# A cross-attention and expert-FFN kernel: its opening rewritten to take tiles in twos, with the query projected right after the first half of the keys

## The chip, the cores and the metric

The kernel runs on one core of a Trainium2 chip. The metric is the device time of one execution in microseconds (us). The engines are TensorE (PE, with its weight loads as PEld), VectorE (DVE), ScalarE (ACT), GpSimd (POOL) and SyncE (SP), whose queue issues all DMAs of this kernel.

## The reference

```python
x = x + xattn(layernorm(x), ctx)         # x: 4 x 512 x 256, ctx: 4 x 1024 x 256
x = x + ffn(layernorm(x))                # 16 experts of 128, gated by a sigmoid
# xattn: lat = LN(x)*g+b; c = LN(ctx)*g+b; q = lat@Wq; k, v = split(c@Wkv)
#        16 heads of 64; k = rope(k, cos, sin)
#        softmax(clip(q k^T / 8, -11, 11)) v, then @Wo + bo
```

Every product of the projections and of the scores is taken as three fp32r products (hi x hi, hi x lo, lo x hi), so each operand is rounded ("hi") and its remainder kept ("lo").

## The kernel before

The attention phase works on 32 items: 4 batches by 8 pairs of heads ("pair" below always means such a pair of heads, item n). While item n runs, its successor p = n + 1 is prepared. An item has four macro steps m, and in each two of its eight score steps s (128 rows of context against 512 queries, for two heads). Every engine has its own order, written out by hand, and semaphores couple them; nothing is planned by a program.

- **PE** (L912 to L956): in m = 0 the scores 0 and 1 of item n, then the two key halves of item n + 1 (`project_k`), then the last two steps of `attend` (probabilities by values) of item n - 1 and its second `denominators`. In m = 1 scores 2 and 3, `q_product(n + 1)`, half of the values (`project_v`), attend 0 and 1. In m = 2 scores 4 and 5, the transposes of one tile of inputs (`turn_tile`), attend 2 and 3. In m = 3 scores 6 and 7, the other half of the values, attend 4 and 5, the first `denominators`.
- **ACT** (L1093 to L1128): the exponentials of each macro step and the copies out of PSUM; in m = 2 `round_k` and then the `affine` of the tile.
- **DVE** (L1308 to L1350): clips each exponential (L1231), adds them in twos (L1239), takes the statistics of tile t = n + 10 in m = 0, normalises it in m = 1 (L1175, L1178), and right behind that turns the denominators of item n - 1 into inverses (`invert_den`, L166 to L172), then the rope products of item n + 1.
- **SP** (L547 to L589), in this order for item n: `swap_k(n + 1)` (4 DMAs), `load_tile(n + 11)`, for n = 1 the load of `x2_head` and of the gate's weights (3 DMAs, L556 to L558), `turn_den(n - 1)` (4 DMAs from `den` to `den_rows`, L156 to L163), `load_weights`, `store_inv`, `spread_inv`, stores of packed weights. What stands behind a wait of this queue waits too. `load_tile(t)` waits until tile t - 2 has been normalised, which frees its buffer `ctx_raw[t % 2]`; tiles with even t also bring one tile of x into the single `x_raw`.
- **POOL** (L711 to L726): in each item `rstd` (a power, L616), `rope_times` (L668), for the first items `split_weights` and `split_v_weights`, then the hi and lo parts of the tile (L631 to L638).

Before item 0 comes the prologue, which is what the change rewrites. It takes the first ten tiles of context (eight make batch 0) and five tiles of x one by one: statistics and normalisation on DVE (L1241 to L1264), the power on POOL, transposes on PE (`turn_first`, L867), the scale and shift and the hi parts on ACT (`affine_first`, L983), the lo parts on POOL (`split_first`, L618). Between them stand, on PE (L889 to L910), the key half 0 of item 0, the value products 0 and 1, the key half 1, the query, the value products 2 and 3. A key half is copied to SBUF (`evac_k`), its rows are swapped in blocks of 32 by DMA (`swap_half`, L495), multiplied and added (`rope_first`, L670 on POOL and L1212 on DVE), and then rounded and split (`round_k_first`, `split_k_first`). The first scores need the first key half, scores 4 to 7 the second (L823, L828). The weights of items 0 and 1 are rounded on ACT and split on DVE; from item 2 on POOL does both.

## Time and profile before

| | |
|---|---|
| median of three runs | 1074.72 us (1074.5 to 1076.34) |
| the profiled execution: its own time | 1075.38 us |
| its span in the profile | 1073.6 us |
| PE busy | 1019.8 us (95% of the span) |
| DVE busy | 777.9 us (72%) |
| ACT busy | 525.4 us (49%) |
| POOL busy | 354.6 us (33%) |
| mean granted PE clock | 0.992 |

Times in the rows count from the span's start, which is also the zero of all times in the text. The profiled execution took 0.66 us more than the median of the three runs, and 1.78 us more than its own span.

### The profile page before, as it was taken

The numbers are of one execution on the slowest core, as the hardware profiler recorded it, in microseconds if no ns is written. First come the engines' busy times: TensorE is split into PE (matmuls) and PEld (weight loads), VectorE is DVE, ScalarE is ACT, GpSimd is POOL, SyncE is SP. The second block draws the span as 40 slices with busy tenths as digits, with TensorE's granted clock in tenths as the row PEclk, the third lists the DMA queues.
The fourth block names the chain that finished last, engine by engine and source line by source line (L and its number), as shares of the span: only waits on it lengthen the run. The fifth ranks groups of instructions, "written<-read, shape, count | busy, mean of one in ns | idle before, by whom it ended". The sixth has DMA issues, their size and how long they took to land. (4 is left out here: it accounts for less than half of the span.)

```text
span 1073.6 us, 15789 instructions
## 1 busy us (share of the span) xinstructions
PE 1019.8 (95%) x5592; PEld 612.8 (57%) x5592; DVE 777.9 (72%) x1140; ACT 525.4 (49%) x759; POOL 354.6 (33%) x276
## 2 busy tenths in 40 slices
PE   4599999999999999999999999999999878999998
PEld 3455455555555555555555555555554356888886
DVE  5498888877888888888888777778778855545422
ACT  5455455555555555655555555555555532222221
POOL 4464534332323222323222211332111145445443
PEclk9899999999999999999999999999999999999999
DMA  6344223332322232323222223322222354332321
GB/s 170 115 137 115 83 85 99 99 96 78 90 65 89 65 90 70 102 80 95 85 70 85 60 80 91 88 79 80 80 60 61 100 181 181 119 109 89 109 108 40
DMA packets 69371, 101.43 MB, mean 94 GB/s; under 512 B 22000, under 2 KB 44784, under 8 KB 67248
## 3 DMA queue, kind: packets, MB, share of 16 engines
q1 hardware_dynamic: 69296, 100.46, 30.8%
q8 instruction: 43, 0.70, 0.3%
q14 instruction: 32, 0.26, 0.1%
HBM read 70.54 MB, written 10.75 MB: 76 GB/s over the span
## 5 line engine op out<-in xcount | busy, mean ns | idle before, releaser
L1026 ACT ACTIVATE probs<-score_ps 128x1024 f32<-128x1024 f32 x256 | 248.8, 1025 | 202.6 <-PE score_ps L835 202.5
L1231 DVE TENSOR_SCALAR probs<-probs 128x1024 f32<-128x1024 f32 x256 | 233.1, 932 | 142.1 <-ACT probs L1026 142.0
L848 PE MATMUL o_ps<-probs,v_sb 128*64 128x512 f32 x1024 | 249.5, 608 | 0.0
L1239 DVE TENSOR_TENSOR p_sum<-probs 128x1024 f32<-128x1024 f32 x128 | 164.7, 1287 | 3.3
L668 POOL TENSOR_TENSOR k_swap<-k_swap,sin_sb 128x1024 f32<-128x1024 f32 x31 | 89.0, 2870 | 189.9 <-DMA k_swap<-k 189.9
L848 PEld LDWEIGHTS o_ps<-probs,v_sb 128*64 128x64 f32 x1024 | 62.3, 136 | 113.1 <-issue 87.6
L835 PE MATMUL score_ps<-q_hi,k_hi 64*128 64x512 f32 x512 | 114.8, 444 | 1.2 <-DVE k_lo L1210 0.8
L1543 POOL TENSOR_TENSOR act_lo<-act,act_hi 128x512 fp32r<-128x512 f32 x64 | 82.6, 1292 | 99.1 <-ACT act_hi L1691 99.1
L835 PEld LDWEIGHTS score_ps<-q_hi,k_hi 64*128 64x128 f32 x512 | 48.3, 184 | 112.5 <-issue 104.5
L1775 DVE SCALAR_TENSOR_TENSOR act<-h_ps,sel_all 128x512 f32<-128x512 f32 x62 | 42.8, 691 | 94.6 <-PE h_ps L142 82.8
L1691 ACT CAST act_hi<-act 128x512 fp32r<-128x512 f32 x64 | 39.7, 622 | 139.5 <-DVE act L1775 139.5
L835 PE MATMUL score_ps<-q_lo,k_hi 64*128 64x512 f32 x512 | 101.4, 391 | 0.0
L835 PE MATMUL score_ps<-q_hi,k_lo 64*128 64x512 f32 x512 | 101.2, 390 | 0.0
L616 POOL TENSOR_TENSOR rstd_sb<-var_sb,power 128x2 f32<-128x2 f32 x32 | 30.8, 961 | 164.0 <-DVE var_sb L1165 96.3
L631 POOL CAST wide_hi<-ctx_t 128x256 fp32r<-128x256 f32 x22 | 24.0, 1093 | 157.9 <-ACT x_t L979 80.5
L142 PE MATMUL job_ps<-wv_hi,wide_hi 128*128 128x256 f32 x240 | 70.8, 295 | 0.0
L863 PE MATMUL side_ps<-p_sum,ones 128*32 128x512 f32 x512 | 68.2, 604 | 0.4 <-DVE yT L218 0.4
L142 PE MATMUL job_ps<-wv_hi,wide_lo 128*128 128x256 f32 x240 | 67.9, 283 | 0.0
L142 PE MATMUL job_ps<-wv_lo,wide_hi 128*128 128x256 f32 x240 | 67.8, 282 | 0.0
L142 PE MATMUL job_ps<-wide_hi,w_hi 128*128 128x512 f32 x128 | 55.1, 430 | 2.8 <-POOL wide_lo L621 2.8
L835 PEld LDWEIGHTS score_ps<-q_lo,k_hi 64*128 64x128 f32 x512 | 48.3, 184 | 11.1
L1018 ACT CAST k_hi<-k 128x1024 fp32r<-128x1024 f32 x31 | 32.5, 1049 | 40.4 <-DVE k L1205 40.4
(196 smaller groups left out, 1898.0 us busy)
## 6 DMA issues: line engine op xcount, KB each, us to landing
sel_all<-sel_dram SPq DMA_DIRECT2D x16, 1024.0 KB, 5.0
k_swap<-k SPq DMA_DIRECT2D x124, 128.0 KB, 2.3
w_hi<-packs_hi SPq DMA_DIRECT2D x26, 384.0 KB, 3.9
w_lo<-packs_lo SPq DMA_DIRECT2D x26, 384.0 KB, 4.4
den<-inv_dram SPq DMA_DIRECT2D x64, 128.0 KB, 2.8
ctx_raw<-ctx SPq DMA_DIRECT2D x24, 128.0 KB, 2.2
packs_hi<-w_hi SPq DMA_DIRECT2D x8, 384.0 KB, 3.3
packs_lo<-w_lo SPq DMA_DIRECT2D x8, 384.0 KB, 3.6
```

What stands on the lines that cost most here:

```text
L142: mm = pe.matmul(out, lhsT, rhs, start=start and i == 0, stop=stop and i == len(terms) - 1)
L668: pool.tensor_tensor(k_swap[:], k_swap[:], sin_sb[:], ALU.mult).then_inc(k_times, 1)
L835: mm = pe.matmul(score_ps[s % 2][:, h, :], k[par][rows, s * P:(s + 1) * P], q[par][rows, :], start=(i == 0), stop=(i == len(terms) - 1))
L848: mm = pe.matmul(o_ps[DH * h:DH * h + DH, :], v_sb[n // 2 % 2][:, at:at + DH], probs[s % RING][:, h, :], start=(s == 0), stop=(s == STEPS ...
L863: mm = pe.matmul(side_ps[at:at + QUAD, :], ones[:], p_sum[2 * part + e][:, h, :], start=(part == 0), stop=(part == 1))
L1018: act.copy(k_hi[p % 2][:], k32[:]).then_inc(k_hi_done, 1)
L1026: act.activation(probs[s % RING][:], score_ps[s % 2][:], ACT.Exp, scale=DH ** -0.5).then_inc(exp_done, 1)
L1231: dve.tensor_scalar(probs[s % RING][:], probs[s % RING][:], CLIP_HI, CLIP_LO, ALU.min, ALU.max).then_inc(clipped, 1)
L1239: dve.tensor_tensor(p_sum[m][:], first, second, ALU.add).then_inc(summed_up, 1)
L1543: pool.tensor_tensor(act_lo[e % ARING][:], act32[e % ARING][:], act_hi[e % ARING][:], ALU.subtract).then_inc(act_split, 1)
L1691: act.copy(act_hi[e % ARING][:], act32[e % ARING][:]).then_inc(act_hi_done, 1)
L1775: dve.scalar_tensor_tensor(out=act32[e % ARING][:], in0=h_ps[e % ARING][:], scalar=0.0, in1=gates[:, at:at + 512], op0=ALU.max, op1=ALU.mu ...
```

## The change

Five changes go together. (1) The first ten tiles of context are handled as five twos ("duos"), with one semaphore step for each: two tiles of context, and in duos 0 and 1 also two tiles of x, so that the four tiles of x that batch 0 needs come in the first two duos. Transposes fill whole banks, and `affine_first` and `split_first` work on blocks of 256 columns twice, or 512 elements in one instruction. (2) The fifth tile of x, which came with tile 8, now comes with tile 11 (`LATE_X`), within item 1; `load_tile(11)` and `load_tile(12)` therefore wait until the tile before them has been normalised as a whole. (3) The order on PE is: duos 0, 1 and 2 turned, value product 0, key half 0, the query, duo 3, value product 1, key half 1, value products 2 and 3. (4) The fifth duo is turned, scaled, rounded and split within item 0 on PE, ACT and POOL, and the second key half is rounded within item 0. (5) DVE takes over the rounding of item 0's weights from ACT; on SP the value weights are loaded behind tiles 4 to 7, the swap of key half 0 goes ahead of the loads of the next weights, and the swap of key half 1 goes behind those loads and the stores of the packed weights.

```diff
--- before
+++ after
...
+LATE_X = 11
...
+FIRST_DUOS = FIRST_TILES // 2
...
+    u = t - FIRST_TILES
+    return u + (u + 1) // 2 + (1 if t > LATE_X else 0)
...
+
+        first_cn = [x2_head[:, 2 * i:2 * i + 2, :] for i in range(2)]
+        first_xn = [t[:].rearrange("p (i d) -> p i d", d=D) for t in (den, o_raw)]
+        first_ct = [yT[:, 0, i * NQ:(i + 1) * NQ].rearrange("p (k n) -> p k n", k=KT) for i in range(2)]
+        first_xt = [yT[:, 1, i * NQ:(i + 1) * NQ].rearrange("p (k n) -> p k n", k=KT) for i in range(2)]
 
         key_raw = [w_raw, w_raw, k_swap, cos_sb]
...
+        def x_index(tile):
+
+            return STEPS // 2 if tile == LATE_X else tile // 2
+
         def x_at(t, tile):
 
-            i = tile % STEPS // 2
-            return t[:, tile // STEPS % 2, :, i * P:(i + 1) * P]
+            i = x_index(tile)
+            return t[:, i // PER % 2, :, i % PER * P:(i % PER + 1) * P]
 
         def has_x(tile):
 
-            return tile % 2 == 0
+            return tile % 2 == 0 or tile == LATE_X
...
+        def duo_x(d):
+
+            return d < PER // 2
...
+        def duo_banks(d):
+
+            if d < 2:
+                return score_ps[d][:, 0, :], score_ps[d][:, 1, :]
+            return (o_ps if d == 2 else side_ps)[:], None
...
+            if f < 2:
+                return score_ps[1][:, f, :]
             if f < FILLS:
...
             def load_tile(t):
 
                 if t >= FIRST_TILES:
-                    sp.wait_ge(normed, blocks(t - 1))
+                    sp.wait_ge(first_normed, FIRST_DUOS)
+                    wait(sp, normed, blocks(t if t in (LATE_X, LATE_X + 1) else t - 1))
                 sp.dma_start(ctx_raw[t % 2][:], ctx_in[t * P:(t + 1) * P, :]).then_inc(ctx_loaded[t % 2], DMA)
...
+            for i in range(2):
+                two = slice(2 * i, 2 * i + 2)
+                sp.dma_start(rows_c[0][:, two, :], ctx_in[2 * i * P:(2 * i + 2) * P, :].rearrange("(t p) d -> p t d", p=P)
+                             ).then_inc(rows_loaded[i], DMA)
+                sp.dma_start(rows_x[:, two, :], x[2 * i * P:(2 * i + 2) * P, :].rearrange("(t p) d -> p t d", p=P)
+                             ).then_inc(rows_loaded[i], DMA)
+                if i == 0:
+                    sp.dma_start(col_sb[:], cols).then_inc(cols_loaded, DMA)
             load_weights(0)
-            load_v_weights(0)
             sp.dma_start(rows_c[1], ctx_in[4 * P:8 * P, :].rearrange("(t p) d -> p t d", p=P)
                          ).then_inc(rows_loaded[2], DMA)
+            load_v_weights(0)
             for q in range(4):
                 rows = slice(32 * q, 32 * q + 32)
                 sp.dma_start(cos_sb[rows, :], cosT).then_inc(consts_loaded, DMA)
                 sp.dma_start(sin_sb[rows, :], sinT).then_inc(consts_loaded, DMA)
             load_tile(8)
             load_tile(9)
+            swap_half(0)
             load_weights(1)
             load_v_weights(1)
-            swap_half(0)
-            swap_half(1)
             store_pack(0)
             store_v_pack(0)
+            swap_half(1)
             load_tile(FIRST_TILES)
             load_weights(2)
...
+                    sp.wait_ge(first_turned, FIRST_DUOS)
                     sp.dma_start(x2_head[:], x[0:512, :].rearrange("(t p) d -> p t d", p=P)).then_inc(head_loaded, DMA)
...
+            def rstd_first(d):
+
+                pool.wait_ge(first_stats, d + 1)
+                wait(pool, first_normed, d - 1)
+                w = 4 if duo_x(d) else 2
+                pool.tensor_tensor(first_rstd[d % 2][:, 0:w], first_var[d % 2][:, 0:w], power[:, 0:w],
+                                   ALU.pow).then_inc(first_rstd_ready, 1)
...
+            def split_first(d):
+
+                pool.wait_ge(first_hi, d + 1)
+                last = pool.tensor_tensor(duo_cols(ctxT_lo, d), first_ct[d % 2], duo_cols(ctxT_hi, d), ALU.subtract)
+                if duo_x(d):
+                    last = pool.tensor_tensor(xT_lo[:, 0, :, d * DUO:(d + 1) * DUO], first_xt[d % 2],
+                                            xT_hi[:, 0, :, d * DUO:(d + 1) * DUO], ALU.subtract)
+                last.then_inc(first_split, 1)
...
-            for t in range(STEPS):
-                rstd(t)
-                if t >= 2:
-                    split_first(t - 2)
-                if t == 6:
-                    pool.wait_ge(sin_signed, 2)
-                    rope_first(0)
-            split_first(STEPS - 2)
-            rstd(STEPS)
-            split_first(STEPS - 1)
-            rstd(STEPS + 1)
+            rstd_first(0)
+            rstd_first(1)
+            split_first(0)
+            rstd_first(2)
+            split_first(1)
+            rstd_first(3)
+            split_first(2)
+            split_first(3)
+            pool.wait_ge(sin_signed, 2)
+            rope_first(0)
+            rstd_first(4)
             rope_first(1)
...
+                    pe.wait_ge(first_split, FIRST_DUOS if p >= PAIRS else STEPS // 2)
+                    if p >= PAIRS:
+                        pe.wait_ge(tile_split, blocks(STEPS * (p // PAIRS + 1)))
...
-                    pe.wait_ge(tile_split, blocks(STEPS * (2 * j // PAIRS + 1)))
+                    if j >= DUOS:
+                        pe.wait_ge(first_split, FIRST_DUOS)
+                        pe.wait_ge(tile_split, blocks(STEPS * (2 * j // PAIRS + 1)))
...
-                    pe.wait_ge(affine_done, blocks(FIRST_TILES))
+                    pe.wait_ge(v_stored, 2)
...
+            def turn_first(d):
+
+                pe.wait_ge(first_normed, d + 1)
+                c_bank, x_bank = duo_banks(d)
+                for bank, rows in ((c_bank, first_cn[d % 2]), (x_bank, first_xn[d % 2])):
+                    if bank is not None:
+                        for k in range(KT):
+                            for i in range(2):
+                                tr = pe.transpose(bank[:, (2 * k + i) * P:(2 * k + i + 1) * P],
+                                                  rows[:, i, k * P:(k + 1) * P], ident[:])
+                tr.then_inc(first_turned, 1)
...
-            for t in range(5):
-                turn_first(t)
-            pe.wait_ge(tile_split, blocks(4))
+            turn_first(0)
+            turn_first(1)
+            turn_first(2)
+            pe.wait_ge(first_split, 1)
+            pe.wait_ge(wv_split, 1)
+            pe.wait_ge(first_affine, 2)
+            v_product(0, 0)
+            pe.wait_ge(first_split, 2)
             pe.wait_ge(w_split, 1)
             k_product(0, 0)
-            turn_first(5)
-            pe.wait_ge(wv_split, 1)
-            v_product(0, 0)
-            turn_first(6)
+            q_product(0)
+            turn_first(3)
             v_product(0, 1)
-            turn_first(7)
-            pe.wait_ge(tile_split, blocks(8))
+            pe.wait_ge(first_split, 4)
+            pe.wait_ge(q_split, 1)
             k_product(0, 1)
-            pe.wait_ge(k_evac, 1)
-            q_product(0)
-            turn_first(STEPS)
-            pe.wait_ge(v_stored, 1)
             v_product(0, 2)
-            turn_first(STEPS + 1)
-            pe.wait_ge(v_stored, 2)
+            pe.wait_ge(first_affine, 4)
             v_product(0, 3)
...
+                    if n == 0 and m == 1:
+                        pe.wait_ge(v_stored, FILLS)
+                        turn_first(FIRST_DUOS - 1)
...
+            def affine_first(d):
+
+                act.wait_ge(first_turned, d + 1)
+                wait(act, first_split, d - 1)
+                c_bank, x_bank = duo_banks(d)
+                for k in range(KT):
+                    last = act.activation(first_ct[d % 2][:, k, :], c_bank[:, k * DUO:(k + 1) * DUO], ACT.Identity,
+                                          bias=b_ctx[:, k:k + 1], scale=g_ctx[:, k:k + 1])
+                if duo_x(d):
+                    for k in range(KT):
+                        last = act.activation(first_xt[d % 2][:, k, :], x_bank[:, k * DUO:(k + 1) * DUO], ACT.Identity,
+                                              bias=b_lat[:, k:k + 1], scale=g_lat[:, k:k + 1])
+                last.then_inc(first_affine, 1)
+                act.wait_ge(first_affine, d + 1)
+                last = act.copy(duo_cols(ctxT_hi, d), first_ct[d % 2])
+                if duo_x(d):
+                    last = act.copy(xT_hi[:, 0, :, d * DUO:(d + 1) * DUO], first_xt[d % 2])
+                last.then_inc(first_hi, 1)
...
-            affine_first(0)
-            affine_first(1)
-            round_weights(0)
-            affine_first(2)
-            affine_first(3)
-            round_v_weights(0)
-            affine_first(4)
-            evac_k(0, 0)
-            affine_first(5)
-            store_v(0, 0)
             def round_k_first(half):
                 act.wait_ge(k_roped, half + 1)
                 act.copy(k_half(k_hi[0], half), k_half(k32, half)).then_inc(k_hi_done, 1)
 
-            affine_first(6)
+            affine_first(0)
+            affine_first(1)
+            affine_first(2)
+            store_v(0, 0)
+            evac_k(0, 0)
+            round_q(0)
+            affine_first(3)
             store_v(0, 1)
+            evac_k(0, 1)
             round_k_first(0)
-            affine_first(7)
-            evac_k(0, 1)
-            round_q(0)
-            affine_first(STEPS)
             store_v(0, 2)
+            store_v(0, 3)
             round_weights(1)
-            store_v(0, 3)
-            affine_first(STEPS + 1)
-            round_k_first(1)
...
+                    if n == 0 and m == 0:
+                        round_v_weights(1)
+                        round_k_first(1)
+                    if n == 0 and m == 1:
+                        affine_first(FIRST_DUOS - 1)
...
+            def stats_first(d):
+
+                slot, width = d % 2, 4 if duo_x(d) else 2
+                if d < 2:
+                    dve.wait_ge(rows_loaded[d], 2 * DMA)
+                elif d < FIRST_DUOS - 1:
+                    dve.wait_ge(rows_loaded[2], DMA)
+                else:
+                    for i in range(2):
+                        dve.wait_ge(ctx_loaded[i], DMA)
+                rows = duo_rows(d)
+                if duo_x(d):
+                    rows = rows + [rows_x[:, 2 * d + i, :] for i in range(2)]
+                for i in range(width):
+                    last = dve.bn_stats(first_bn[slot][:, i, :], rows[i])
+                last.then_inc(first_bn_done, 1)
+                dve.wait_ge(first_bn_done, d + 1)
+                for i in range(width):
+                    last = dve.bn_aggr(first_mv[slot][:, i, :], first_bn[slot][:, i, :])
+                last.then_inc(first_aggregated, 1)
+                dve.wait_ge(first_aggregated, d + 1)
+                wait(dve, first_rstd_ready, d - 1)
+                last = dve.tensor_scalar(first_var[slot][:, 0:2], first_mv[slot][:, 0:2, 1], EPS, None, ALU.add)
+                if duo_x(d):
+
+
+                    last = dve.tensor_scalar(first_var[slot][:, 2:4], first_mv[slot][:, 2:4, 1], 1.0 + EPS, EPS * EPS,
+                                             ALU.mult, ALU.add)
+                last.then_inc(first_stats, 1)
...
+            def normalize_first(d):
+
+                slot = d % 2
+                dve.wait_ge(first_rstd_ready, d + 1)
+                wait(dve, first_turned, d - 1)
+                for i, rows in enumerate(duo_rows(d)):
+                    last = dve.tensor_scalar(first_cn[slot][:, i, :], rows, first_mv[slot][:, i, 0:1],
+                                             first_rstd[slot][:, i:i + 1], ALU.subtract, ALU.mult)
+                if duo_x(d):
+                    for i in range(2):
+                        last = dve.tensor_scalar(first_xn[slot][:, i, :], rows_x[:, 2 * d + i, :],
+                                                 first_mv[slot][:, 2 + i, 0:1], first_rstd[slot][:, 2 + i:3 + i],
+                                                 ALU.subtract, ALU.mult)
+                last.then_inc(first_normed, 1)
+
+            def round_weights():
+
+                dve.wait_ge(w_loaded, 3 * DMA)
+                dve.tensor_copy(w_hi[0][:], w_raw[:, 0:WC]).then_inc(w_hi_done, 2)
+                split_weights(0)
+
+            def round_v_weights():
+
+                dve.wait_ge(wv_loaded, DMA)
+                dve.tensor_copy(wv_hi[0][:], wv_raw[:]).then_inc(wv_hi_done, 1)
+                split_v_weights(0)
...
-                    rope_first(1)
+            stats_first(0)
+            normalize_first(0)
+            stats_first(1)
+            normalize_first(1)
+            stats_first(2)
+            round_weights()
+            normalize_first(2)
+            stats_first(3)
+            round_v_weights()
+            normalize_first(3)
+
+            dve.wait_ge(consts_loaded, 8 * DMA)
+            for q in (0, 2):
+                rows = slice(32 * q, 32 * q + 32)
+                dve.tensor_scalar(sin_sb[rows, :], sin_sb[rows, :], -1.0, None, ALU.mult).then_inc(sin_signed, 1)
+            split_q(0)
+            stats_first(4)
+            rope_first(0)
+            split_k_first(0)
+            normalize_first(4)
+            rope_first(1)
             split_weights(1)
             split_k_first(1)
             split_v_weights(1)
                             invert_gate(dve, sh, 0, 0)
...
+                            wait(dve, turned, t - FIRST_TILES)
                             normalize(t, ctx_n[:], x_n[:])
                         if n > 0:
                             invert_den(dve, sh, n - 1)
...
```

## Rows read from the trace of the kernel before

**Rows 1.** Busy time by stretch: us of PE, PEld, DVE, ACT, POOL; then PEclk, DMA share, GB/s.

```profile
0.00:25.00 25.00, 9.75 (x33) 7.12 (x34) 15.29 (x59) 13.33 (x32) 13.36 (x25) 1.00 0.65 175
25.00:50.00 25.00, 13.91 (x69) 11.85 (x69) 10.61 (x22) 10.00 (x23) 10.10 (x11) 0.80 0.32 101
50.00:75.00 25.00, 23.13 (x140) 13.49 (x137) 22.93 (x29) 16.03 (x26) 16.70 (x14) 1.00 0.51 167
200.00:825.00 625.00, 625.00 (x3624) 343.75 (x3622) 502.54 (x675) 347.63 (x475) 154.40 (x98) 1.00 0.28 82
```

**Rows 2.** PE in order of time: start, us of the group, what, count, idle before.

```profile
8.15 0.66 PE L751 MATMUL score_ps<-ident,x_head 128*128 128x128 f32 x2 [8.15 <-DVE den L1178]
8.61 0.63 PE L754 MATMUL score_ps<-ident,den 128*128 128x128 f32 x2
...
22.96 0.56 PE L142 MATMUL o_ps<-wv_hi,wide_hi 128*128 128x256 f32 x1
25.66 0.42 PE L751 MATMUL score_ps<-ident,x_head 128*128 128x128 f32 x2
...
34.95 0.80 PE L142 MATMUL job_ps<-wide_hi,w_hi 128*128 128x512 f32 x1 [2.17 <-POOL wide_lo L621]
...
46.25 0.69 PE L751 MATMUL score_ps<-ident,x_head 128*128 128x128 f32 x2 [4.35 <-DVE x_head L1175]
49.43 0.59 PE L835 MATMUL score_ps<-q_hi,k_hi 64*128 64x512 f32 x2
```

**Rows 3.** DVE in order of time, prologue and item 0.

```profile
3.34 0.43 DVE L1150 BATCH_NORM_STATS2 bn_c<-probs 128x6 f32<-128x256 f32 x1 [3.34 <-DMA p_sum<-x]
3.68 0.41 DVE L1152 BATCH_NORM_STATS2 bn_x<-p_sum 128x6 f32<-128x256 f32 x1
...
44.37 1.10 DVE L1219 TENSOR_TENSOR k<-k,k_swap 128x512 f32<-128x512 f32 x1
...
53.51 0.27 DVE L1270 MEMSET sel_lo<- 128x256 f32 x1
...
60.41 2.48 DVE L1175 TENSOR_SCALAR ctx_n<-ctx_raw,mv_c,rstd_sb 128x256 f32<-128x256 f32 x1
```

**Rows 4.** POOL in order of time.

```profile
11.67 0.72 POOL L621 TENSOR_TENSOR wide_lo<-x_head,wide_hi 128x256 fp32r<-128x256 f32 x1 [1.54 <-ACT xT_hi L992]
13.69 1.36 POOL L621 TENSOR_TENSOR wide_lo<-x_head,wide_hi 128x256 fp32r<-128x256 f32 x1
59.95 2.79 POOL L668 TENSOR_TENSOR k_swap<-k_swap,sin_sb 128x1024 f32<-128x1024 f32 x1 [1.27 <-DMA k_swap<-k]
```

**Rows 5.** Stretches of 2 us, columns as in the first group.

```profile
4.00:6.00 2.00, 0.00 (x0) 0.00 (x0) 0.61 (x6) 0.00 (x0) 0.71 (x1) 1.00 1.07 367
46.00:48.00 2.00, 1.75 (x8) 1.75 (x9) 1.06 (x2) 0.00 (x0) 0.04 (x1) 0.56 0.20 68
118.00:120.00 2.00, 2.00 (x6) 0.48 (x4) 1.97 (x4) 0.60 (x1) 0.00 (x0) 0.50 0.03 4
```

**Rows 6.** SP's DMA issues within item 1, first and last of nine.

```profile
80.70 0.58 SPq L445 DMA_DIRECT2D ctx_raw<-ctx  x1
...
83.31 2.46 SPq L163 DMA_DIRECT2D den_rows<-den  x4
```

**Rows 7.** The tile `den_rows`: from issue to landing, over 12 DMAs.

```profile
DMA to landing us min/median/max: 1.8/1.9/2.8
```

**Rows 8.** DVE within item 1.

```profile
87.90 1.91 DVE L1175 TENSOR_SCALAR ctx_n<-ctx_raw,mv_c,rstd_sb 128x256 f32<-128x256 f32 x1
89.73 0.15 DVE L170 TENSOR_TENSOR inv_rows<-den_rows 128x8 f32<-128x8 f32 x1
92.40 1.29 DVE L1231 TENSOR_SCALAR probs<-probs 128x1024 f32<-128x1024 f32 x2
```

**Rows 9.** PE within item 1 and at the start of item 2.

```profile
95.32 1.94 PE L848 MATMUL o_ps<-probs,v_sb 128*64 128x512 f32 x8
98.18 0.50 PE L835 MATMUL score_ps<-q_hi,k_hi 64*128 64x512 f32 x2
```

129 lines of the change are left out of this document (42 added, 87 removed).

## The prediction

> **What bounds the kernel now.** I read the stretches first [rows 1]. From 200 to 825 us PE is busy all 625 us at full clock, so there a microsecond is neither won nor lost by the opening: whatever item 2 starts earlier or later should come out at the end. In the first 50 us PE is busy 23.7 us (9.75 + 13.91), much of it slowly. That is what the change can win from. PE in order of time [rows 2] shows the opening as one long chain: first transposes at 8.15, value product 0 at 22.96 (12 matmuls in 2.7 us, to 25.66), key half 1 at 34.95 (6 matmuls of 512, as many columns in all), an idle 4.35 us before 46.25 while DVE ropes key half 1, and the first scores at 49.43. The second thing to see is that DVE, not PE, paces item 0: it has 22.93 us of work in the 25 us from 50 [rows 1]. So I follow DVE too: its last preparation ends at 53.7 and it normalises tile 10 at 60.41 [rows 3].
>
> **Part 1, duos up to the first product.** The first duo needs 512 KB where two transfers of 128 KB were enough. Data for the old first tile was there at 3.34 [rows 3]; the stretch from 4 to 6 us moves 367 GB/s [rows 5], so 256 KB more take 0.7 us, and I take 4.8 with the extra issues. DVE: four statistics 0.34 us apart [rows 3] and the small ones, 2.05 in all; POOL's power, 0.75, which has no cover now, since DVE's next statistics stand behind the normalisation; four normalisations, 1.4: 9.0. Eight transposes at twice the 1.1 us of four [rows 2]: 11.1. ACT's four affines of 256 columns have no row. Those of 128 come 0.35 apart; between the same and double I take 0.45, 1.9 us together, then two casts of 512 elements, 1.1 us: 14.2. POOL's two splits of 512 elements: one of 256 takes 0.72 alone and 1.36 beside DVE's weight split [rows 4], so 2.6 alone, and with DVE's weight work beside them 3.8: 18.0. Then the power of duo 2 (0.7), which stands behind that split, DVE's normalisation of duo 2 (20.7, held by POOL's next split), statistics of duo 3, and the value weights, rounded and split by DVE: 23.1. The two casts that DVE takes over have no row there either: between 0.3 and 1.0 us each, near the DVE operations of their size, 0.7 taken. ACT's saving of them costs nothing, for ACT waits there.
>
> So value product 0 starts at 23.1, as before (22.96). **The gain comes behind it.** Key half 0 follows directly (as many columns at the same pace, 2.6 taken, to 28.4), the query (1.8, to 30.2), duo 3, value product 1 (to 32.1). Duo 3 goes through ACT (32.4) and POOL (33.7), key half 1 takes 1.4 at full clock (35.1), value products 2 and 3 1.4 each: 37.9. The first key half is swapped by 33.1, roped by 35.9, split by 37.2, all within that. The first scores at 37.9 against 49.43 [rows 2].
>
> **Part 2, the second key half and item 0.** Its copy is ready at 35.7. SP has by then issued the 4 weight loads and 4 stores it is moved behind; their 1.9 MB take 5.2 us at the rate above, from 31.5 to 36.9, and 8 issues of about half a microsecond. I put its landing at 40.2. Rope: DVE done at 42.3, against 45.5 (44.37 + 1.10 [rows 3]). Then the weight split of item 1 (43.2), ACT's rounding of the half, its split (43.9), value weights, memsets: DVE is free for item 0 at 45.2 against 53.8, 8.6 us earlier. PE waits for item 1's weights from about 40 to 43.2. After its idle 4.35 us the clock stood at 0.56 from 46 to 48 [rows 2, 5]; if this gap does the same, the two key halves of item 1 take up to 5.2 us instead of 2.8, the query is late, and so are duo 4 on ACT and POOL, behind which stand POOL's power of tile 10 and its rope product. Then DVE reaches tile 10 at 54.2, 6.2 us earlier; without it, 8.5. The added transposes (0.5 us), affines and split of duo 4 cost PE nothing while DVE paces. I take a gain of **7.5**, with 5.5 and 9.5 as ends.
>
> **Part 3, the x tile that moves to item 1.** The work only moves: 0.5 us of statistics, which fall into an idle of DVE, and one normalisation. The wait does not. `load_tile(12)` now waits on SP until tile 11 is normalised as a whole, which DVE does in m = 1 of item 1. Behind it in SP's queue stand the three head loads and the four transfers of `turn_den(0)`; and the next instruction on DVE is `invert_den(0)`, which waits for those four. In the old frame: DVE ends tile 11 at 89.7, with x at 90.4 [rows 8]. SP then issues what took it from 80.70 to 85.77, 5.07 us [rows 6], and the last of the four transfers lands some 1.9 behind its issue [rows 7]: 97.3. `invert_den(0)` stood at 89.73 [rows 8]: DVE is 7.5 us late, and had no wait there before. Its next clips end at 93.7 [rows 8] and will end at 101.2. PE goes on alone: transposes, attend 2 and 3, scores 6 and 7, value product, to 96.0; attend 4 was at 95.32 [rows 9] and can start when the first of those clips is done, 100.6. PE loses **5.3 us**, idle for 4.6. Item 2's scores (98.18 [rows 9]) come as late: k must be split by DVE, at 103.6. And after an idle of 4.35 us in the opening the clock was low until 49.6, which doubled 3.4 us of work: I add **1.7**, with 0 and 2.9 as ends (the value product at 22.96 was still at half pace after the gaps before it [rows 2], the longest such stretch here). Together 7.0.
>
> **Sum.** -7.5 + 5.3 + 1.7 = -0.5; and the old trace has one more low stretch, 0.50 from 118 to 120 in item 2 [rows 5], behind a short wait for DVE. It cost some 1.7 us and may not come back in another timing; I take off 0.3 for that: -0.8. Against the profiled execution's own 1075.38 that is 1074.6; it ran 0.66 above the median of the runs, so 1073.9 against 1074.72. What a measurement here can tell from no change is about 0.2%, 2.1 us.
>
> **The rule on the shared port.** DVE's normalisation of tile 10, 256 elements, took 2.48 us from 60.41, and POOL's rope product ran from 59.95 to 62.74 [rows 3, 4]: DVE waited it out. The Trainium skill ("SBUF — State Buffer", Who interferes with whom) says as much: a copy, cast or tensor_scalar of DVE in a 2-port mode and a GpSimd operation exclude each other for the whole instruction. This trace agrees, with those 2.48 us. Taken strictly, every normalisation, cast or weight split of the new opening that meets a split of POOL waits for its whole 1.3 us, which is the first rival below with its 1078.7; by the costs above it is 1073.9.
>
> **Rivals.**
> - *The hold in the opening* (slower). POOL's splits double in length, and each now stands where DVE normalises the next duo or rounds weights. I counted one such hold (1.3 us) and 1.2 us on POOL. If duos 2, 3 and the key half each meet two more splits or products, 2.6 us are added before value product 0, and as much around the rope, the gain falls to about 3.0, and 7.0 are lost later: +4.0, so 1078.7. It decides from the point where the gain falls under 4.9. For it: the 1.36 and the 2.48 [rows 3, 4]. Against it: POOL is idle for half of the old opening (13.36 of 25 [rows 1]).
> - *The stall in item 1 is covered* (faster). If DVE's invert isn't held, or PE has more queued than I count, the gain stays: -6 to -9, about -7.5, so 1067.2. Against it: the orders of SP and DVE are fixed, and nine issues behind a wait can't be early. For it: PE's margin, that I could only count to 96.0.
> - *The chain is as costed* (my forecast): from -4.0 to +2.5, 1070.7 to 1077.2.
>
> **How the numbers follow.** Forecast 0.62: of it 0.36 within 0.2%, 0.18 faster, 0.08 slower. The covered stall 0.25, all faster. The hold 0.13: 0.09 slower, 0.04 within. So faster 0.43, same 0.40, slower 0.17. The range leaves out 0.1 at either end: 1067.5 to 1077.5.
>
> **What would show it.** First scores near 38 (35 to 40). Value product 0 near 23. DVE's clip of step 0 near 45, and normalisation of tile 10 near 53. In item 1 SP silent between `swap_k` and `load_tile(12)` until DVE has normalised x of tile 11, then DVE idle some 6.8 us before `inv_rows`, PE idle 4 to 5 us before attend 4, and a low granted clock behind. I am wrong if that idle isn't there, or if scores of item 2 start by more than 3 us earlier than 98.18.

## The result, and the profile after

The changed kernel takes 1078.03 us (median of six, 1077.45 to 1081.56), against 1074.99 for the kernel before in the same session (six, 1074.31 to 1076.72): a ratio of 1.0032, 95% interval [1.0016, 1.0048]. It is slower by some 3.0 us, where 1073.9 had been forecast and the range ended at 1077.5. (A ratio here and below is not exactly the quotient of the two medians, which would be 1.0028.) One run of those below, 1154.91 us of the kernel with a filler, was in a slow state and counts in no ratio. The profiled execution was the longest of the six, 1081.56 with a span of 1079.8. At 841 us it is 2.3 us behind the kernel before and at its end 6.2, so most of what it has above the median arises behind 841 us, and times up to there can be read as they stand.

The stretches of the kernel after, columns as in [rows 1]:

```profile
0.00:25.00 25.00, 7.13 (x30) 5.99 (x31) 17.12 (x48) 9.26 (x17) 12.18 (x19) 1.00 0.54 142
25.00:50.00 25.00, 17.00 (x88) 13.81 (x89) 14.59 (x29) 10.47 (x18) 5.11 (x5) 0.86 0.52 170
...
200.00:825.00 625.00, 623.89 (x3617) 342.97 (x3613) 505.84 (x680) 347.85 (x474) 154.49 (x99) 1.00 0.28 81
...
44.00:46.00 2.00, 1.39 (x3) 1.17 (x4) 2.00 (x5) 0.29 (x1) 0.00 (x0) 0.50 0.12 33
46.00:48.00 2.00, 2.00 (x6) 1.60 (x5) 1.97 (x4) 0.45 (x1) 0.00 (x0) 0.50 0.89 305
...
98.00:100.00 2.00, 2.00 (x6) 0.24 (x2) 2.00 (x3) 2.00 (x5) 1.01 (x1) 0.50 0.72 269
...
122.00:124.00 2.00, 2.00 (x7) 0.27 (x4) 1.98 (x3) 1.19 (x2) 0.00 (x0) 0.50 0.26 96
...
850.00:875.00 25.00, 21.47 (x97) 9.76 (x94) 16.05 (x21) 9.65 (x12) 3.66 (x3) 0.86 0.27 73
875.00:900.00 25.00, 18.42 (x68) 14.38 (x67) 9.99 (x30) 6.06 (x10) 17.04 (x13) 0.80 0.69 236
```

From 200 to 825 us PE is still full (623.89 of 625 us), so the opening's account is closed by then. Three low stretches are to be seen: at 44 to 48, at 98 to 100, and at 122 to 124 us. The third is the old one of item 2, which the kernel before has from 118 to 120 [rows 5]. The last two lines belong to the surplus of this execution: the kernel before had a granted clock of 1.00 in both of those stretches. It is the only one of all twelve traces that had, though, so its end is as much an exception as this one.

PE in order of time, columns as in [rows 2]:

```profile
22.89 0.55 PE L144 MATMUL score_ps<-wv_hi,wide_hi 128*128 128x256 f32 x1 [1.14 <-issue]
...
36.66 0.51 PE L886 MATMUL score_ps<-q_hi,k_hi 64*128 64x512 f32 x2
...
44.61 0.77 PE L144 MATMUL job_ps<-wide_hi,w_hi 128*128 128x512 f32 x1 [6.28 <-issue]
...
49.87 0.51 PE L886 MATMUL score_ps<-q_hi,k_hi 64*128 64x512 f32 x2
...
69.93 0.51 PE L886 MATMUL score_ps<-q_hi,k_hi 64*128 64x512 f32 x2 [0.76 <-DVE k_lo L1327]
...
97.10 3.38 PE L899 MATMUL o_ps<-probs,v_sb 128*64 128x512 f32 x8 [4.23 <-DVE probs L1348]
100.41 1.26 PE L914 MATMUL side_ps<-p_sum,ones 128*32 128x512 f32 x8
101.60 0.50 PE L886 MATMUL score_ps<-q_hi,k_hi 64*128 64x512 f32 x2
```

The same stations in the kernel before, as far as [rows 2] do not have them:

```profile
72.96 0.51 PE L835 MATMUL score_ps<-q_hi,k_hi 64*128 64x512 f32 x2 [0.77 <-DVE k_lo L1210]
...
97.19 1.07 PE L863 MATMUL side_ps<-p_sum,ones 128*32 128x512 f32 x8
```

Read against the kernel before: value product 0 at 22.89 (22.96), first scores at 36.66 (49.43, so 12.8 earlier), scores of item 1 at 69.93 (72.96, 3.0 earlier), scores of item 2 at 101.60 (98.18, 3.4 later). Three stations: 12.8 won; 9.8 of it gone within item 0 (5.3 of these because DVE reaches its first clip only 7.5 earlier; the forecast had 2.9 of that, 11.5 against 8.6); another 6.4 gone within item 1. What is left is a kernel that is 3.4 late. The first `denominators` of item 1, the line at 100.41, come 3.2 us later than in the kernel before. In the item near 232 us it is still 3.2 (235.25 against 232.03), and in the one near 841 us 2.3 (841.02 against 838.74). I use the line of item 1 as milestone **D1** below (before 97.19, after 100.41), since it stands behind both losses.

DVE and POOL, columns as in [rows 3, 4]:

```profile
41.14 1.78 DVE L1334 TENSOR_TENSOR k<-k,cos_sb 128x512 f32<-128x512 f32 x1 [4.46 <-DMA k_swap<-k]
...
43.56 0.95 DVE L1301 TENSOR_TENSOR w_lo<-w_raw,w_hi 128x768 fp32r<-128x768 f32 x1
...
46.18 1.22 DVE L1348 TENSOR_SCALAR probs<-probs 128x1024 f32<-128x1024 f32 x2
...
51.94 0.69 DVE L1348 TENSOR_SCALAR probs<-probs 128x1024 f32<-128x1024 f32 x1 [2.02 <-ACT probs L1092]
...
54.90 0.69 DVE L1312 TENSOR_TENSOR q_lo<-job_ps,q_hi 128x512 fp32r<-128x512 f32 x1 [1.35 <-ACT q_hi L1071]
...
57.42 2.45 DVE L1229 TENSOR_SCALAR ctx_n<-ctx_raw,mv_c,rstd_sb 128x256 f32<-128x256 f32 x1 [0.59 <-POOL rstd_sb L656]
...
86.69 0.40 DVE L1232 TENSOR_SCALAR x_n<-x_raw,mv_x,rstd_sb 128x256 f32<-128x256 f32 x1
93.67 0.17 DVE L172 TENSOR_TENSOR inv_rows<-den_rows 128x8 f32<-128x8 f32 x1 [6.59 <-DMA den_rows<-den]
...
96.36 1.29 DVE L1348 TENSOR_SCALAR probs<-probs 128x1024 f32<-128x1024 f32 x2
```

```profile
54.46 1.29 POOL L669 TENSOR_TENSOR wide_lo<-yT,wide_hi 128x512 fp32r<-128x512 f32 x1 [12.09 <-ACT wide_hi L1055]
55.70 1.68 POOL L656 TENSOR_TENSOR rstd_sb<-var_sb,power 128x2 f32<-128x2 f32 x1
57.35 2.36 POOL L716 TENSOR_TENSOR k_swap<-k_swap,sin_sb 128x1024 f32<-128x1024 f32 x1
```

SP's issues, in the opening and in item 1, columns as in [rows 6]:

```profile
30.45 0.59 SPq L494 DMA_DIRECT2D w_raw<-Wq  x1
...
34.20 1.21 SPq L525 DMA_DIRECT2D v_packs_lo<-wv_lo  x1
35.46 3.87 SPq L539 DMA_DIRECT2D k_swap<-k  x4
...
75.20 2.42 SPq L548 DMA_DIRECT2D k_swap<-k  x4
87.16 0.34 SPq L484 DMA_DIRECT2D ctx_raw<-ctx  x1
...
89.98 2.45 SPq L165 DMA_DIRECT2D den_rows<-den  x4
```

**Item 1 went as forecast.** SP is silent from the swap at 75.20 until `x_n` of tile 11 is done, some 87.1; nine issues follow; the four transfers of `turn_den(0)` are the last; DVE's `inv_rows` waits 6.59 us for them; the clips that attend 4 waits for move to 96.36, PE is idle 4.23 and then goes at half clock.

**Item 0 did not.** DVE was to be free for the clip of step 0 at 45.2 and is at 46.18, 7.5 earlier than before. But from there to tile 10 DVE took 11.2 us where it had taken 6.7, from this line of the kernel before to 60.41 [rows 3]:

```profile
53.71 1.22 DVE L1231 TENSOR_SCALAR probs<-probs 128x1024 f32<-128x1024 f32 x2
```

The lines of the changed kernel name the waits: 2.02 for ACT's probabilities, 0.22 for the next, 1.35 for ACT's `q_hi`, 0.59 for POOL's power, 4.2 together. They lead back to PE, whose keys of item 1 began at 44.61. PE's row names no releaser for its 6.28 us, but the split of their weights ends on DVE just before (`w_lo`, 43.56 and 0.95). It stands behind the rope on DVE, and the rope behind the swap on SP. An experiment below tests this.

### The profile page after: what moved, and what is told of

It reads as the page before. It is cut to its first block and busy times, and to the rows that moved or that the text cites. A ratio compares the mean times of both kernels' runs of the same rounds, so it can differ in the third digit from the quotient of the medians.

```text
span 1079.8 us, 15769 instructions
## 1 busy us (share of the span) xinstructions
PE 1022.3 (95%) x5592; PEld 614.0 (57%) x5592; DVE 779.2 (72%) x1125; ACT 518.8 (48%) x735; POOL 350.8 (32%) x265
## 5 line engine op out<-in xcount | busy, mean ns | idle before, releaser
L899 PE MATMUL o_ps<-probs,v_sb 128*64 128x512 f32 x1024 | 252.7, 615 | 4.2 <-DVE probs L1348 4.2
L656 POOL TENSOR_TENSOR rstd_sb<-var_sb,power 128x2 f32<-128x2 f32 x22 | 24.0, 1090 | 148.5 <-DVE var_sb L1222 87.5
```

Source lines behind the costliest of these rows:

```text
L899: mm = pe.matmul(o_ps[DH * h:DH * h + DH, :], v_sb[n // 2 % 2][:, at:at + DH], probs[s % RING][:, h, :], start=(s == 0), stop=(s == STEPS ...
```

## The experiments

Ten kernels were timed in three sessions, each beside the kernel before (1075.42, 1075.62 and 1074.69 us, medians of 23 to 25 runs). Three edits recur: **den** (`turn_den(0)` ahead of the wait), **weights** (item 1's weights split on DVE ahead of the rope) and **swap** (the swap of key half 1 issued on SP ahead of the stores).

Times in a trace are from one execution each. How far they repeat can be read from pairs of kernels that are the same program up to item 1. The scores of item 1 start at 72.96 and 72.90 (the kernel before, without and with the wait), at 69.93 and 69.87 (the changed kernel, without and with **den**), and in the three other such pairs 0.5, 0.7 and 1.0 us apart. A difference under 1 us in one trace therefore says little.

### The wait in item 1: taken away, and alone

**den**, on the changed kernel (SP, item 1):

```diff
+                if n == 1:
+                    turn_den(sp, sh, n - 1)
                 if n + FIRST_TILES + 1 < TILES:
                     load_tile(n + FIRST_TILES + 1)
...
-                if n > 0:
+                if n > 1:
                     turn_den(sp, sh, n - 1)
```

> The changed kernel, with turn_den(0) issued on SP ahead of load_tile(12) and the head loads in item 1; all else as it is. Theory (the transfers behind the new wait hold DVE and then PE): DVE's idle 6.59 us before inv_rows and PE's 4.23 us before attend 4 are gone, no low clock follows, and of the 6.4 us that item 1 loses (3.0 ahead at its start, 3.4 behind at its end) 5 to 7 come back: 1071 to 1073 us, item 2 starting about 3 us earlier than in the kernel before. Rival (item 1 is slower because of the x tile moved into it, not because of the wait): at most 1 us comes back, 1077 us.

Measured 1071.34 (7 runs), ratio 0.9965 [0.9945, 0.9984]: 6.7 us under the changed kernel, as the theory had it, and faster than before. DVE and PE of this kernel:

```profile
86.51 0.40 DVE L1234 TENSOR_SCALAR x_n<-x_raw,mv_x,rstd_sb 128x256 f32<-128x256 f32 x1
86.83 0.15 DVE L172 TENSOR_TENSOR inv_rows<-den_rows 128x8 f32<-128x8 f32 x1
...
92.62 1.94 PE L901 MATMUL o_ps<-probs,v_sb 128*64 128x512 f32 x8
94.49 1.07 PE L916 MATMUL side_ps<-p_sum,ones 128*32 128x512 f32 x8
```

No wait on either engine, attend 4 in 1.94 instead of 3.38 us, D1 5.9 earlier. `load_tile(12)` itself goes out as late as in the changed kernel (86.99 against 87.16), and DVE never waits for it.

The other way round, the kernel before with the wait alone (tile 12 waits for the whole of tile 11; no other part of the change):

```diff
-                    sp.wait_ge(normed, blocks(t - 1))
+                    sp.wait_ge(normed, blocks(t if t == 12 else t - 1))
```

> The kernel before, with one edit: load_tile(12) waits until tile 11 has been normalised, as in the changed kernel; no x tile is moved. Theory (the wait alone costs it): DVE idle 6 to 7 us before inv_rows in item 1, PE idle 4 to 5 us and a stretch at low clock: 6 to 7 us slower than before, 1081 to 1082 us. Rival (the moved tile costs it): within 1 us of before, 1075 us.

Measured 1082.98 (6 runs), ratio 1.0065 [1.0044, 1.0085], 7.6 us over the kernel before in its session and 1 us more than the theory's 1081 to 1082:

```profile
96.51 0.17 DVE L170 TENSOR_TENSOR inv_rows<-den_rows 128x8 f32<-128x8 f32 x1 [6.77 <-DMA den_rows<-den]
...
99.94 3.68 PE L848 MATMUL o_ps<-probs,v_sb 128*64 128x512 f32 x8 [4.61 <-DVE probs L1231]
```

One changed condition in one wait reproduces the whole stall, with D1 6.4 later (103.55 against 97.19). No tile of x is moved here, so the stall is not owed to tile 11's bigger load.

### The keys of item 1: at full clock, or earlier

A filler on PE in the gap (24 matmuls of 512 columns whose result nobody reads):

```diff
+                    if n == 0 and m == 0:
+                        pe.wait_ge(v_stored, 3)
+                        for r in range(4):
+                            product(pe, o_ps[:], split_terms(0, 1, ctx_cols(ctxT_hi, 0, 0),
+                                                             ctx_cols(ctxT_lo, 0, 0)))
                     if m == 0 and p < NPAIR:
                         project_k(p, 0)
                         project_k(p, 1)
```

> The changed kernel, with 24 matmuls of 512 columns more on PE, into o_ps, whose result nobody reads, right behind the first two score steps of item 0: they fill some 5.6 us of the idle 6.3 us before the keys of item 1. Theory (the low clock after that gap costs 2.4 us on PE, and the delay passes through the query, ACT and POOL to the normalisation of tile 10): the two key halves take 2.8 us instead of 5.3, item 1 starts 1.5 to 2.5 us earlier, 1075.5 to 1076.5 us. Rival (DVE's own queue paces item 0, the clock doesn't): item 1 starts within 0.5 us of now, 1078 us.

Measured 1078.13 (12 runs), ratio 1.0014 [0.9993, 1.0035], so the time is the rival's; D1 at 101.26, not earlier than 100.41. PE's keys and DVE of this kernel:

```profile
45.35 0.47 PE L144 MATMUL job_ps<-wide_hi,w_hi 128*128 128x512 f32 x1 [0.56 <-issue]
...
46.92 1.22 DVE L1353 TENSOR_SCALAR probs<-probs 128x1024 f32<-128x1024 f32 x2
...
55.85 0.41 DVE L1234 TENSOR_SCALAR ctx_n<-ctx_raw,mv_c,rstd_sb 128x256 f32<-128x256 f32 x1 [0.59 <-POOL rstd_sb L656]
...
56.51 3.40 DVE L1323 TENSOR_TENSOR k<-k,cos_sb 128x1024 f32<-128x1024 f32 x1
```

The keys ran at full clock (granted 1.00 from 44 to 50 us), although like the clip they began 0.7 later. From the clip of step 0 to tile 10 DVE took 8.9 us, against 11.2 in the changed kernel and 6.7 before: with the keys just as late, the clock alone is worth 2.3 of the 4.5 us that item 0 lost there. Tile 10 came 1.6 earlier and the scores of item 1 at 68.56, 1.4 earlier. The 1.4 was lost at once: those scores and the keys behind them met a low clock of their own (0.75 from 68 to 70 and 0.50 from 70 to 72 us, where the changed kernel had 1.00), after PE had been busy only 2.07 us of the four from 64 to 68. ACT's copy of the next key half comes at 73.36 against 73.23, so the two kernels are level there. What the filler gained was gone one item later.

**weights**, on the changed kernel (DVE):

```diff
             normalize_first(4)
-            rope_first(1)
             split_weights(1)
-            split_k_first(1)
             split_v_weights(1)
+            rope_first(1)
+            split_k_first(1)
```

> The changed kernel, with DVE splitting the weights of item 1 (keys, query, values) ahead of its rope of key half 1 instead of behind it. Theory (PE's 6.3 us before the keys of item 1 are a wait for w_lo, which stands on DVE behind the late swap, and the low clock follows from that idle time): the keys of item 1 start near 39 instead of 44.6, at full clock; tile 10 is normalised 2 to 4 us earlier and item 1 starts 2 to 4 us earlier: 1074 to 1076 us. Rival (the late swap itself paces item 0 through DVE, so that the keys of item 1 come early for nothing): item 1 starts within 1 us of now, 1077 to 1078 us.

Measured 1076.43 (12 runs), ratio 1.0006 [0.9991, 1.0022], between the theory's 1074 to 1076 and the rival's 1077. The trace is the theory's. The keys of item 1 began at 39.85. The clip of step 0 was no earlier (46.10), and from there to tile 10 DVE took 7.7 us instead of 11.2: tile 10 was normalised at 53.78 instead of 57.42. So this one order holds 3.6 of the 4.5 us. The scores of item 1 came 2.2 earlier and D1 1.8 (98.60), so half of the 3.6 was given back. Beside that loss there is a new gap: PE had run ahead, was idle 4.00 us before tile 10's transposes and ran on at a granted clock of 0.50 from 56 to 60 us. What share of the loss this gap has wasn't tried.

**swap**, on the changed kernel (SP):

```diff
+            swap_half(1)
             store_pack(0)
             store_v_pack(0)
-            swap_half(1)
```

> The changed kernel with the swap alone moved ahead of the stores. Theory (the missing gain of item 0 is the late swap, through DVE's rope and, behind it, the weights of item 1 and PE's idle time): the keys of item 1 start 2 to 2.5 us earlier than 44.6 and item 1 2 to 3 us earlier than 69.9; 1075 to 1076 us. Rival (it is the low clock and the fifth duo): under 1 us, 1077 to 1078 us.

Measured 1079.23 (10 runs), ratio 1.0028 [1.0003, 1.0052]; the 1075 to 1076 of the theory were missed. In the trace the clip of step 0 and the keys are each 1.05 earlier (45.13 and 43.56), item 1's scores 1.5 and D1 1.3 (99.11), about half of what was expected; in the time nothing of it can be told from the spread. The gap before the keys stays, 4.85 us.

### The edits together

**den** with **weights**:

> The changed kernel with both edits: turn_den(0) ahead of load_tile(12), and item 1's weights split ahead of the rope of key half 1. Theory (two separate losses, one after the other on the path): e1 stands 6.7 us under the changed kernel and e3 1.6, so 8 to 9 us under it, 1069 to 1070.5 us, about 5 us under the kernel before. Rival (DVE paces items 0 and 1, so the earlier weights bring nothing once the other wait is gone): as e1, 1071.3 us.

Measured 1071.02 (12 runs), ratio 0.9959 [0.9943, 0.9975]; D1 91.39. The trace is 3.1 us ahead of **den** alone, as the theory had it, but the median is the rival's: 0.3 under it.

**den** with **swap**:

> The changed kernel with two edits: turn_den(0) ahead of load_tile(12) on SP, and the swap of key half 1 ahead of the stores of the packed weights of item 0. The split of item 1's weights stays behind the rope. Theory A (the swap's lateness costs something by itself, by way of the normalisation of tile 10): the first denominators of item 1 start at 93.2 (94.49 with the first edit alone, less the 1.3 that the swap edit gave by itself), the time is 1070.0. Theory B (the keys of item 1, which wait for the weights, are what holds item 0, and the swap only matters because the weights' split stands behind the rope that it releases; then the two edits give as much as the earlier keys, about 1.0): 93.5 and 1070.3. Rival C (the swap is hidden): 94.5 and 1071.3, as with the first edit alone. A and B are told from C by the denominators' start, and A from B by the gap of PE before the keys of item 1: still 4.5 to 5 us with a low granted clock behind it.

Measured 1070.91 (12 runs), ratio 0.9958 [0.994, 0.9977]; D1 92.47, earlier than any of the three had it, while the gap before the keys stayed (4.69 us), the sign of theory A. But the keys themselves began 1.9 us earlier than with **den** alone (43.15 against 45.08), so this run does not separate A from B, and its time is not told from that of **den** alone. Better evidence are the pairs in which the weights already stand ahead and only the swap changes: there D1 comes 1.3 earlier (98.60 to 97.33) and 0.9 (91.39 to 90.49). That the swap's lateness counts by itself is likely, but no larger than the traces repeat.

**weights** with **swap**, the wait left in:

> The changed kernel with the split of item 1's weights ahead of the rope of key half 1 on DVE, and the swap of key half 1 ahead of the stores; the wait of load_tile(12) stays in front of turn_den(0). Theory A (the two losses are independent, each in its own stage): the time is that of the kernel with all three edits, 1067.4, plus the 6.4 to 7.1 of the wait: 1073.8 to 1074.5, the same as before the change; the first denominators of item 1 start at 96.5 to 97.5, against 90.49 with all three. Rival B (the wait hides what the opening wins, since SP's queue and DVE then meet in item 1 whatever came before): no better than the weights' edit alone, 1076.4, and denominators at 98.6.

Measured 1075.20 (12 runs), ratio 1.0006 [0.9986, 1.0025]; D1 97.33, within the 96.5 to 97.5 of theory A. With the opening mended and the wait left in, the kernel is just where it was before the change. The median lies 0.7 above A's range of times and 1.2 under B's; the denominators, 1.3 from B's, speak for A.

All three edits:

> e5, with the swap of key half 1 issued on SP ahead of the four stores of packed weights (behind the four weight loads as now). Theory (what DVE starts item 0 by is the late landing of that swap): the swap lands near 38.5 instead of 41.1, DVE clips step 0 near 44 instead of 46.1, item 1 starts 1.5 to 2.5 us earlier than in e5: 1067 to 1068.5 us. Rival (the stores, now later, meet the loads of tile 10 and of the next weights, or SP is late for them): no better than e5.

Measured **1067.39** (6 runs), ratio 0.9921 [0.9892, 0.995]: the lowest median of all, 8.2 us under the kernel before and some 10.6 under the changed one. The time is in the theory's range, but the trace is only 0.9 us ahead of **den** with **weights**, where 1.5 to 2.5 were expected, so part of the 3.6 between the two medians is spread. POOL, DVE and PE of this kernel:

```profile
49.18 1.29 POOL L671 TENSOR_TENSOR wide_lo<-yT,wide_hi 128x512 fp32r<-128x512 f32 x1 [7.96 <-ACT wide_hi L1057]
50.44 1.14 POOL L658 TENSOR_TENSOR rstd_sb<-var_sb,power 128x2 f32<-128x2 f32 x1
53.66 2.36 POOL L718 TENSOR_TENSOR k_swap<-k_swap,sin_sb 128x1024 f32<-128x1024 f32 x1 [2.08 <-DMA k_swap<-k]
```

```profile
38.79 0.96 DVE L1303 TENSOR_TENSOR w_lo<-w_raw,w_hi 128x768 fp32r<-128x768 f32 x1 [1.44 <-ACT w_hi L1110]
...
45.01 1.23 DVE L1350 TENSOR_SCALAR probs<-probs 128x1024 f32<-128x1024 f32 x2
...
52.68 0.40 DVE L1231 TENSOR_SCALAR ctx_n<-ctx_raw,mv_c,rstd_sb 128x256 f32<-128x256 f32 x1
...
53.69 3.42 DVE L1320 TENSOR_TENSOR k<-k,cos_sb 128x1024 f32<-128x1024 f32 x1 [0.28 <-DMA k_swap<-k]
```

```profile
39.85 0.47 PE L144 MATMUL job_ps<-wide_hi,w_hi 128*128 128x512 f32 x1 [0.86 <-issue]
```

The weights split at 38.79 in the time that DVE used to wait for the swap, the keys follow at once, and POOL reaches the power 5.3 us earlier. Tile 10 comes at 52.68, a quarter of a microsecond from the 52.9 that a gain of 7.5 had meant. From the clip of step 0 to there it is still 7.7 us, where the kernel before had 6.7. The fifth duo's work on ACT (1.04 and 0.62) and POOL (1.29) lies in this stretch now; whether that is the last 1.0 us was not tried. ctx_n no longer meets POOL's rope product, but the rope on DVE now does (3.42 where it took 1.52 in the changed kernel).

**Clips early**, on **den** with **swap**, moves more of DVE's order: zeroing of `sel_hi` and `sel_lo`, item 1's weights and the first two clips ahead of the rope of key half 1.

```diff
             normalize_first(4)
-            rope_first(1)
-            split_weights(1)
-            split_k_first(1)
-            split_v_weights(1)
-
             dve.memset(raw(sh.sel_hi), 0.0).then_inc(sel_zero, 1)
             dve.memset(raw(sh.sel_lo), 0.0).then_inc(sel_zero, 1)
+            split_weights(1)
+            clip(0, 0)
+            clip(0, 1)
+            split_v_weights(1)
+            rope_first(1)
+            split_k_first(1)
...
-                    clip(n, 2 * m)
-                    clip(n, 2 * m + 1)
+                    if n > 0 or m > 0:
+                        clip(n, 2 * m)
+                        clip(n, 2 * m + 1)
```

> e6, with DVE's two memsets and its clips of score steps 0 and 1 of item 0 also ahead of the rope of key half 1, where DVE idles for some 4 us in the changed kernel. Theory (DVE's own queue paces item 0): 1 to 2 us under e6, 1066 to 1067 us. Rival (the clips push the rope and the second key half later by as much): as e6 or slower.

Measured 1069.09 (8 runs), ratio 0.994 [0.9918, 0.9962], D1 90.14 against 90.49: the clip of step 0 starts at 39.30 instead of 45.01 and still tile 10 at 52.66 instead of 52.68. The time and the trace are the rival's; nothing more is to be had there.

**The eight combinations side by side**, and the kernel before. In each cell the first number is with the wait ahead of `turn_den(0)`, the second without it. The third column of times is the first `denominators` of the item near 841 us, behind the long stretch in which PE is full.

| weights, swap | scores of item 1 | D1 | near 841 us | ratio |
|---|---|---|---|---|
| none | 69.93, 69.87 | 100.41, 94.49 | 841.02, 833.16 | 1.0032, 0.9965 |
| weights | 67.71, 66.67 | 98.60, 91.39 | 837.67, 830.09 | 1.0006, 0.9959 |
| swap | 68.45, 67.72 | 99.11, 92.47 | 838.56, 831.34 | 1.0028, 0.9958 |
| both | 66.22, 65.77 | 97.33, 90.49 | 837.16, 829.13 | 1.0006, 0.9921 |
| kernel before | 72.90, 72.96 | 103.55, 97.19 | 844.57, 838.74 | 1.0065, 1 |

From the scores of item 1 to D1 every kernel of the table with the wait takes 30.5 to 31.1 us and every one without it 24.2 to 24.8: the wait costs 5.9 to 6.4 there, whatever the opening. Near 841 us it is 5.8 in the kernel before and 7.2 to 8.0 in the others. By the ratios it is 0.0047 to 0.0085, that is 5.1 to 9.1 us of time. Part of what comes behind D1 is the old low stretch of item 2. It is there in the traces of the kernel before, the changed one and **swap**, and in none of the five with **den**; from D1 to the denominators near 232 us the first two take 134.8 us and those five 133.0 to 133.1.

The two reorderings together are worth 3.7 and 4.1 us at the scores of item 1, and 3.9 and 4.0 near 841 us. So the wait and the opening are nearly independent losses. The reorderings are not independent of each other: near 841 us they give 3.4 and 2.5 one by one with the wait, 5.8 if they added up, and 3.9 together. The medians show less of a gain than the traces near 841 us, by 0.7 to 4.0 us: what happens behind 841 us differs from execution to execution, and whether the opening has a part in it was not looked into.

## Why the prediction was wrong

**Part 1 (duos up to the first product): right.** First data 4.63 against 4.8, value product 0 at 22.89 against 23.1, first scores 36.66 against 37.9: a gain of 12.8 there where 11.5 was forecast.

**Part 2 (the second key half and item 0): this step failed.** The gain taken was 7.5 with ends of 5.5 and 9.5; it was 3.0, at tile 10 (57.42 against 60.41) and at the scores of item 1 alike. The swap and the rope were sized 1 us short: clip of step 0 at 46.18 against 45.2, so a gain of 7.5 there instead of 8.6. Wrong was what followed, where another 4.5 went. I had written that PE "waits for item 1's weights from about 40 to 43.2", and I gave this wait a price only through the clock: 6.2 of gain if the gap made it low, 8.5 if not. The wait itself was put at 0.1, with no reason given. It lasted from 38.3 to 44.61, 6.3 us instead of 3.2, the keys then took 5.3 us (5.2 forecast for the cold case), and it drew with it ACT's exponentials, `q_hi` and duo 4, POOL's split of duo 4 and, behind that on POOL, the power for tile 10. Those are the 4.2 us of DVE's waits shown above.

The runs take the 4.5 apart, all by DVE's time from the clip of step 0 to tile 10 (6.7 before, 11.2 in the changed kernel). With the gap filled it is 8.9, so the low clock was worth 2.3, which is just the difference between the two cases. With **weights**, which ends the wait, it is 7.7: 1.3 more for the lateness itself. The last 1.0 stays with all three edits, and its cause is open. (Each of these is from one execution and good to half a microsecond: the same stretch took 7.1 in the kernel before with the wait and 10.7 in the changed kernel with **den**, which change nothing up to there; with the weights ahead it was 7.7 in all four kernels of the table.) So there were two errors. The lateness of the keys was priced at next to nothing; and the low clock, which the old trace shows behind its idle 4.35 us, was averaged away, 7.5 being nearer to 8.5 than to 6.2. That the cause lies in the two orders is shown by **weights** and **swap**: they change nothing else, and with both tile 10 stands 7.3 and 7.7 us ahead of the kernel before, where 7.5 was forecast. With all three edits D1 is 6.7 earlier than in the kernel before (90.49 against 97.19), within the ends that I had given this step.

**Part 3 (the x tile moved to item 1): right.** 7.0 forecast, made of 5.3 and 1.7; the changed kernel loses 6.4 between the scores of item 1 and those of item 2, the wait alone costs 7.6 us in the kernel before, and taking it away gives 6.7. DVE idle 6.59 (6.8 forecast), PE idle 4.23 (4.6), clock 0.50 behind it.

**The sum.** With 3.0 in place of 7.5, Part 3 as forecast gives 3.0 of gain against 7.0 of loss, +4.0; measured with 6.4 it is +3.4 at the scores of item 2, +2.3 near 841 us and +3.0 in the medians. The 0.3 taken off for the old low stretch at 118 us has nothing to show for it: the stretch came again 4 us later (0.50 from 122 to 124, with 0.83 before and 0.81 behind it). And the ends of the forecast were added up loosely: its own terms give -4.5 and +2.4, not -4.0 and +2.5. Neither moves the result.

**The rivals.** *The hold in the opening* gave 1078.7 and is nearest in number, but its mechanism is not what happened: value product 0 was not late. Holds there were (a hold: one of DVE and POOL waits out the other's instruction): three on DVE, 2.9 us together, which is about what the forecast had counted. The rival had the condition right (a gain under 4.9) and the place wrong. DVE's splits of the same 768 weights show the hold itself: 0.95 at 43.56 with POOL idle, and 1.90 in this row. It starts within POOL's split at 15.85 and ends 0.8 us behind that one's end; POOL's power, which starts within it, is in turn long (1.41, where the next takes 0.81):

```profile
15.85 1.65 POOL L671 TENSOR_TENSOR xT_lo<-yT,xT_hi 128x512 fp32r<-128x512 f32 x1
16.41 1.90 DVE L1301 TENSOR_TENSOR w_lo<-w_raw,w_hi 128x768 fp32r<-128x768 f32 x1
17.46 1.41 POOL L663 TENSOR_TENSOR first_rstd<-first_var,power 128x2 f32<-128x2 f32 x1
```

The Trainium skill's rule ("SBUF — State Buffer", Who interferes with whom), that such a pair excludes one another for the whole instruction, fits these 1.90 us and the 2.45 of ctx_n; but the 2.6 us more that the rival added before value product 0 were not there. *The stall is covered* fell: DVE's idle before `inv_rows` was there, 6.6 to 7.1 us, wherever the wait stood in front of `turn_den(0)`.

## What to carry to other kernels

When a step is moved, look on every in-order queue for what stands behind the new wait and is already ready: here the turn of the denominators on SP, and the split of the next weights on DVE, were both ready and both stood behind a wait that did not concern them. Moving them ahead, with the swap, made of a kernel 3.0 us slower than before one that is 8.2 faster. And follow a gain to the stage where PE is full before counting it: 12.8 us at the first scores were 3.0 one item later. If a late engine feeds a chain, price each link of the chain, also the ones that had slack before, and price the lateness itself beside the low clock that may follow it. What is won by filling a gap has to be looked for an item later, too.

## What the runs showed of the hardware

- SP's four issues of the swap of key half 1 took 3.87 us, where those of the first half took 2.53 and those of a whole key in item 1 2.42. The same program up to there gave 3.26 with **den**. Over the ten kernels with the new opening it is 2.95 (filler) to 3.87 with the stores ahead and 3.24 to 3.66 with the stores behind, so the stores ahead don't set it, and it differs between executions of one order; what sets it stays open. The forecast had half a microsecond for an issue, 2.0 for four.
- A hold between DVE and POOL was moved rather than removed: with the filler and with the three edits ctx_n fell from 2.45 to 0.41 and 0.40 us, and the next rope on DVE rose from 1.52 to 3.40 and 3.42. From tile 10 to the first scores of item 1 it was 12.5 us in the changed kernel, 12.7 with the filler and 13.1 with all three edits.
- A gap of PE closed by moving work earlier can open another: with **weights**, PE stood idle 4.00 us before tile 10 and the granted clock fell to 0.50 there instead of at the keys.
